# A fused reaction-diffusion and LoRA feed-forward kernel: the first rows of layer 2 by way of DRAM, and two neighbour sums on GpSimd

## The chip, the cores and the metric

The kernel runs on one core of a Trainium2 chip. The metric is the device time of one execution in microseconds (us), as the median of several. TensorE does the matrix products, VectorE and ScalarE the elementwise work, GpSimd some of it and the DMAs that accumulate; SyncE (SP) and ScalarE issue plain DMAs.

## The reference

For each of 8 batches, x is 1024 tokens by 512 features. First a stencil, then a feed-forward layer whose weights have a part that depends on the stencil's own rows 1 to 16, then the residual:

```
y  = zX*(x[t,d-1] - 2x + x[t,d+1]) + zY*(x[t-1,d] - 2x + x[t+1,d]) + zR*x*(1 - x)
even, odd = y[1:17:2], y[2:18:2]             # 8 rows each
m1 = (even[:4] outer odd[:4]) as 2048 x 512  # added to W1
m2 = (even[4:] outer odd[4:]) as 512 x 2048  # added to W2
h  = gelu(y @ (W1 + scale*m1).T + b1)
out = x + h @ (W2 + scale*m2).T + b2
```

(Borders are reflected.) All in float32.

## The kernel before

Products are made from float32 values split into a high and a low part (`yh`/`yl`, `W1h`/`W1l`, `W2h`/`W2l`, `gh`/`gl`), three matmuls of 128x512 for each product, in PSUM. y is computed with features on partitions, in eight tiles a batch: tiles 0 to 3 are the first half of the tokens. The hidden dimension goes in pairs i = 0 to 7 of 128 rows for layer 1 (banks `ph`) and in sixteen tiles n for layer 2 (banks `po`). Batches 1 to 7 repeat one loop; batch 0 has an order of its own, written out by hand for each engine, and the semaphores (`wait_ge`, `then_inc`) tie the engines together. Only the beginning of batch 0 is touched.

The beginning of batch 0 goes so:

- TensorE warms up with 17 matmuls (line 663) and then makes the neighbour sums of y's tile 0 (`raw0`, line 580), `even_row(0)`, the sums of tile 1 (`sums1`), `even_row(1)`, waits for `fold0` and does `pair0(0)`, `even_row(2)`, `pair0(1)`, `pair0(2)` and `pair0(3)` (line 601). `pair0(n)` is the float32 product of W1's first pair of blocks with y's tile n, and waits for that tile (`s_tile`). Then come, at line 630, the six steps of the second pair, which wait for the last part of yh (`s_yht`) and for block 1 of W1h (`s_w1hB`), and at line 694 the first tile of layer 2, which waits for `s_w2h` and, once, for `s_rows2`.
- `even_row(j)` (line 594) spreads a row of four times 128 numbers over all partitions. ScalarE makes diagonal matrices `DE` of the numbers (`diagonals(j)`, line 938), and TensorE multiplies a matrix of ones by them. Row 0 is used for W1's first blocks (`fold0` on VectorE, `outer(0,1)` on ScalarE), row 1 for `outer(0,2)` and `outer(0,3)`, row 2 for W2: ScalarE copies it from PSUM into `EB2` (line 960) and `fold(0, 0)` to `fold(0, 3)` on VectorE (line 1298) add its product with `SC` to the raw W2 tiles.
- The numbers are in `SA`, which VectorE computes in six steps (`scalars0`, the last is `s_sc` 6). Layer 2's later rows come from DRAM: `natural` computes the even rows in another layout, SP stores them to `ep_scratch` and loads them back, broadcast to all partitions (`load_EB2`, into `EB2` or `Ts`).
- A tile n of y needs `scaled(0, n)` on ScalarE (line 787), `mul(0, n)` on VectorE, and the sums of the neighbours in features (`sd`, semaphore `s_md`) and in tokens (`st`, `s_mt`), which `fin` and `tile` on VectorE add. For tile 2 VectorE makes the sums itself (`sums0(2)`, lines 1198 and 1199); for tile 3 GpSimd does (`sums3`, lines 507 and 508), once those of tile 2 are done.
- ScalarE's order: the loads of x tiles 0, 2, 3, 4 (`load_x0`), `scaled` 0 and 1, `diagonals(0)`, `scaled` 2, `diagonals(1)`, `outer(0,1)`, `scaled` 3, `diagonals(2)`, `outer(0,2)`, `outer(0,3)`, the parts yh of tiles 0 and 1 (`part0_h`, line 812), the copy into `EB2`, the parts of tiles 2 and 3, then `w1h_plain(1)` (line 848).
- GpSimd's order: the diagonals of the coefficients, `sums3`, and `add_W1(0, i)`, each a DMA that accumulates the raw W1 blocks onto what `outer(0, i)` has written.
- SP's order: the packed parameters, x tile 1, raw W1 and W2 blocks, `xn`, x tiles 5 to 7, `keep_W1(2)` (which waits for the DMA of `add_W1(0,2)`), two W2 tiles, and so on.

The waits behind `fold` for batch 0 are

```
return ((s_rows2, 1), (d_f1, 16), (d_f2, 16), (d_e2, 16))[j]
```

Of the kernel before, what the change touches and what calls it, by code (L numbers as in the profile page):

```python
# [5 lines left out]
def adaln_ffn_kernel(nc: bass.Bass, xT, xs, x, xn, pk, w1, w2, b2, out):  # L6

    f32 = mybir.dt.float32
    f32r = mybir.dt.float32r
    ALU = mybir.AluOpType  # L10
# [2 lines left out]
    B, S, D = 8, 1024, 512  # L13
    NK, NI = 16, 8
    EP = nc.dram_tensor("ep_scratch", (B * 8, D), f32, kind="Internal").ap()
    UV = nc.dram_tensor("uv_scratch", (NI, 2, 128, 512), f32, kind="Internal").ap()
    TD = nc.dram_tensor("td_scratch", (NI, 128, 512), f32, kind="Internal").ap()

    ctx = ExitStack()
    with ctx:  # L20
# [3 lines left out]
        def sems(names):  # L24
            return [ctx.enter_context(nc.semaphore(n)) for n in names.split()]
# [64 lines left out]
        s_yl = sems(" ".join(f"s_yl{s}" for s in range(7)))  # L90
        d_pk, d_N, d_ep, d_xs = sems("d_pk d_N d_ep d_xs")
        d_keep, d_back = sems("d_keep0 d_keep1"), sems("d_back0 d_back1")
        s_rows2, d_f1, d_f2, d_raw0, d_raw1 = sems("s_rows2 d_f1 d_f2 d_raw0 d_raw1")
        d_e1, d_e2, d_td, d_us, d_vs, d_xr, d_xa = sems("d_e1 d_e2 d_td d_us d_vs d_xr d_xa")
        d_x = sems(" ".join(f"d_x{n}" for n in range(9)))
        d_r, d_q, d_w = sems("d_r0 d_r1"), sems("d_q0 d_q1"), sems("d_w0 d_w1 d_w2 d_w3")
# [78 lines left out]
        def x_at(b, n):  # L175
            x_ = Xs[8 if b else n]
            return [x_[:, r:r + 4, c:c + 128] for r, c in ((1, 1), (0, 1), (2, 1), (1, 0), (1, 2))]

        def sums_at(b, n):
            pair = SS if b else s0[:, n - 1 if n < 4 else n - 3, :, :]  # L180
            return four(pair[:, 0, :]), four(pair[:, 1, :])
# [38 lines left out]
        def rows2_done(b, j):  # L220
            if b:
                return d_e2, 16 * (4 * b + j - 2)
            return ((s_rows2, 1), (d_f1, 16), (d_f2, 16), (d_e2, 16))[j]

        def bank_of(b, h, i, lt):
            if h == 0:
# [7 lines left out]
        def _(e):  # L234
# [7 lines left out]
            def load_x0(n):  # L242
                e.dma_start(Xs[n].rearrange("p r s -> p (r s)"), xT[0, n]).then_inc(d_x[n], 16)
# [59 lines left out]
            def keep_W1(i):  # L303
                e.wait_ge(d_r[i % 2], added(0, i))
                e.dma_start(UV[i].rearrange("h p q -> p h q"),
                            R1[:, i % 2, :, :].rearrange("p (h a) q -> p h (a q)", h=2)).then_inc(d_keep[i % 2], 16)
# [45 lines left out]
            load_W2(0, 0)  # L352
            load_W2(0, 1)
            e.dma_start(xr[:, 0:2, :].rearrange("p a q -> p (a q)"), xn).then_inc(d_N, 16)
            for n in (5, 6, 7):
                load_x0(n)
            keep_W1(2)
            load_W2(0, 2)
            load_W2(0, 3)
# [136 lines left out]
        @block.gpsimd  # L496
        def _(e):
            def diagonal(a, v):
                return e.affine_select(DG[:, a, :], v.broadcast_to([128, 128]), [[-1, 128]],
                                       ALU.is_equal, 0.0, base=0, channel_multiplier=1)  # L500

            def sums3():
                mid, up, down, left, right = x_at(0, 3)
                st, sd = sums_at(0, 3)
                e.wait_ge(d_x[3], 16)
                e.wait_ge(s_mt, 1)
                e.tensor_tensor(sd, up, down, ALU.add).then_inc(s_md, 1)
                e.tensor_tensor(st, left, right, ALU.add).then_inc(s_mt, 1)

            def add_W1(b, i):  # L510
                f = i % 2
                e.wait_ge(s_outer, summed(b, i))
                if (b, i) == (0, 1):
                    e.dma_start(flat(UVs[:, 2:4, :]), w1[1], accum_op=ALU.add).then_inc(d_raw1, 16)
                    return
                e.dma_start(flat(R1[:, f, :, :]), w1[i], accum_op=ALU.add).then_inc(d_r[f], 16)

            def top0(b, i):
                f = i % 2
                if (b, i) > (1, 0):  # L520
                    pb, pi = (b, i - 1) if i else (b - 1, 7)
                    e.wait_ge(d_td, 16 * strassen(pb, pi))
                    e.wait_ge(s_w1lT, strassen(pb, pi))
                e.wait_ge(d_r[f], added(b, i))
                e.tensor_tensor(Ts[:, 0:4:2, :], R1[:, f, 0:1, :].broadcast_to([128, 2, 256]), R1[:, f, 1:3, :],  # L525
                                ALU.subtract).then_inc(s_top0, 1)

            def top1(b, i):
                e.wait_ge(s_top0, strassen(b, i))
                e.tensor_tensor(Ts[:, 1, :], Ts[:, 0, :], R1[:, i % 2, 2, :], ALU.subtract).then_inc(s_top1, 1)  # L530

            def top3(b, i):
                e.wait_ge(s_top1, strassen(b, i))
                e.tensor_tensor(Ts[:, 3, :], Ts[:, 1, :], R1[:, i % 2, 3, :], ALU.add).then_inc(s_top3, 1)

            def add_b2(b, h):
                e.wait_ge(d_xr, 16 * (2 * b + h + 1))
                e.dma_start(xr[:, :, :], bass.AP(b2.tensor, 0, [[0, 128], [0, 4], [1, D]]),
                            accum_op=ALU.add).then_inc(d_xa, 16)

            e.memset(ON[:, :], 1.0).then_inc(s_on, 1)
            e.wait_ge(s_on, 1)
            diagonal(2, ON[:, 0:1]).then_inc(s_sel, 1)
            e.wait_ge(d_pk, 16)
            diagonal(1, zt[:, 0, 1:2]).then_inc(s_dg, 1)
            diagonal(0, zt[:, 0, 0:1]).then_inc(s_dg, 1)
            sums3()
            for i in range(1, NI):
                add_W1(0, i)
            add_b2(0, 0)  # L550
            add_W1(1, 0)
            add_W1(1, 1)
            top0(1, 0)
            top1(1, 0)
            top3(1, 0)
            add_b2(0, 1)
            for b in range(1, B):
                for i in range(7):
                    top0(b, i + 1)
                    top1(b, i + 1)  # L560
                    if i < 6:
                        add_W1(b, i + 2)
                    top3(b, i + 1)
                add_b2(b, 0)
                add_b2(b, 1)
                if b + 1 < B:
                    add_W1(b + 1, 0)
                    top0(b + 1, 0)
                    top1(b + 1, 0)
                    top3(b + 1, 0)  # L570
                    add_W1(b + 1, 1)

        @block.tensor
        def _(e):
# [15 lines left out]
            def even_row(j):  # L590
                for c in range(4):
                    e.wait_ge(s_de, 4 * j + c + 1)
                    bank = (ph[1] if c < 2 else po[2], ph[3], po[3])[j]
                    mm = e.matmul(bank[:, 128 * c:128 * c + 128], ON[:, :], DE[:, j, c, :], start=True, stop=True)  # L594
                mm.then_inc(s_row, 1)

# [70 lines left out]
            even_row(1)  # L667
            e.wait_ge(s_fold1, 1)
            pair0(0)
            even_row(2)  # L670
            for n in range(1, 4):
                pair0(n)

# [14 lines left out]
                mm.then_inc(done, 1)  # L688
            for src, w, ready in ((gh, W2h, s_w2h), (gl, W2h, s_glE), (gh, W2l, s_w2l)):
                e.wait_ge(ready, 1)  # L690
                if ready is s_w2h:
                    e.wait_ge(s_rows2, 1)
                for t in range(4):
                    mm = e.matmul(po[t][:, :], src[:, 0, 128 * t:128 * t + 128], w[:, 1, :], start=w is W2h and src is gh,  # L694
                                  stop=False)
# [80 lines left out]
        def _(e):  # L776
# [152 lines left out]
            def load_x0(n):  # L929
                e.dma_start(Xs[n].rearrange("p r s -> p (r s)"), xT[0, n]).then_inc(d_x[n], 16)  # L930


            def diagonals(j):
                e.wait_ge(s_sel, 1)
                e.wait_ge(s_sc, 6)
                for c in range(4):
                    v = SA[:, c, 2 * j:2 * j + 1] if j < 2 else SA[:, 0, 8 + 2 * c:9 + 2 * c]
                    e.activation(DE[:, j, c, :], DG[:, 2, :], ACT.Copy, scale=v).then_inc(s_de, 1)

            load_x0(0)  # L940
            load_x0(2)
            load_x0(3)
            load_x0(4)
            e.wait_ge(d_pk, 16)
            e.activation(junk[:, :], zt[:, 0, 0:1], ACT.Gelu)
            e.wait_ge(s_zc, 3)
            scaled(0, 0)
            scaled(0, 1)
            diagonals(0)
            scaled(0, 2)  # L950
            diagonals(1)
            outer(0, 1)
            scaled(0, 3)
            diagonals(2)
            outer(0, 2)
            outer(0, 3)
            part0_h(0)
            part0_h(1)
            e.wait_ge(s_row, 3)
            e.activation(EB2[:, :, :].rearrange("p a q -> p (a q)"), po[3][:, :], ACT.Copy).then_inc(s_rows2, 1)  # L960
            part0_h(2)
            part0_h(3)
            w1h_plain(1)
# [185 lines left out]
        def _(e):  # L1149
# [44 lines left out]
            def sums0(n):  # L1194
                mid, up, down, left, right = x_at(0, n)
                st, sd = sums_at(0, n)
                e.wait_ge(d_x[n], 16)
                e.tensor_tensor(sd, up, down, ALU.add).then_inc(s_md, 1)
                e.tensor_tensor(st, left, right, ALU.add).then_inc(s_mt, 1)
# [165 lines left out]
            scalars0()  # L1365
            sums1()
            mul(0, 0)
            sums0(2)
            tile0(0)
            fold0()  # L1370
            mul(0, 1)
# [300 lines left out]
```

## Time and profile before

| | |
|---|---|
| median of 3 runs | 1335.46 us (1335.28 to 1336.07) |
| the profiled execution | 1335.95 us |
| its span, first to last instruction | 1334.7 us |
| granted TensorE clock over the span | 1.000 |
| VectorE, ScalarE, GpSimd busy | 1035.7, 794.3, 256.1 us |
| DMA over the span | 253.52 MB, mean 190 GB/s |

The profile is one execution. The busy times are sums over the instructions; a chain of waits follows the work that ended last back to its start. A matmul's own duration (389 ns for 128x512) contains its pipeline, and the next starts before it ends; in the chain each stands with the time that it adds, 0.23 us. Many instructions of batch 0 overlap by some 0.1 us in the same way.

### The profile page before, as it was taken

The numbers are of one execution on the slowest core, as the hardware profiler recorded it, in microseconds if no ns is written. First come the engines' busy times: TensorE is split into PE (matmuls) and PEld (weight loads), VectorE is DVE, ScalarE is ACT, GpSimd is POOL, SyncE is SP. The second block draws the span as 40 slices with busy tenths as digits, with TensorE's granted clock in tenths as the row PEclk, the third lists the DMA queues.
The fourth block names the chain that finished last, engine by engine and source line by source line (L and its number), as shares of the span: only waits on it lengthen the run. The fifth ranks groups of instructions, "written<-read, shape, count | busy, mean of one in ns | idle before, by whom it ended". The sixth has DMA issues, their size and how long they took to land.

```text
span 1334.7 us, 17125 instructions
## 1 busy us (share of the span) xinstructions
PE 1330.6 (100%) x5901; PEld 1100.4 (82%) x5901; DVE 1035.7 (78%) x1775; ACT 794.3 (60%) x1376; POOL 256.1 (19%) x257
## 2 busy tenths in 40 slices
PE   9999999999999999999999999999999999999999
PEld 7888888888888888888888888888888888888887
DVE  8878799858897688976899768996689967665343
ACT  7654567645775566754577546675467754666432
POOL 1000122301232012320132201331022310232000
PEclk9999999999999999999999999999999999999999
DMA  8765377767778577875868667787767866667661
GB/s 245 195 155 151 81 204 213 203 213 204 180 212 196 189 213 198 203 197 197 208 188 223 183 215 196 193 218 180 224 179 205 214 181 207 161 187 167 176 190 55
DMA packets 140070, 253.52 MB, mean 190 GB/s; under 512 B 13648, under 2 KB 37456, under 8 KB 139984
## 3 DMA queue, kind: packets, MB, share of 16 engines
q1 hardware_dynamic: 121888, 201.03, 47.0%
q0 software_dynamic: 17520, 49.81, 22.5%
q10 hardware_dynamic: 576, 1.60, 0.3%
q8 instruction: 46, 0.75, 0.2%
q14 instruction: 40, 0.33, 0.1%
HBM read 189.34 MB, written 63.05 MB: 189 GB/s over the span
## 4 chain that ended last, share of the span: by engine, by line
PE 100%; DVE 0%; issue 0%; DVEq 0%
PE po L636 17%; PE po L638 17%; PE po L637 17%; PE ph L624 15%; PE ph L620 15%; PE ph L622 15%; PE ph L601 1%; PE ph L630 0%; PE po L580 0%; PE ph L663 0%; PE po L694 0%; DVE xr L1362 0%; PE po L594 0%; PE ph L594 0%; PE po L586 0%; PE po L588 0%
## 5 line engine op out<-in xcount | busy, mean ns | idle before, releaser
L636 PE MATMUL po<-W2h,gh 128*128 128x512 f32 x1020 | 396.8, 389 | 0.0
L637 PE MATMUL po<-W2l,gh 128*128 128x512 f32 x1020 | 396.8, 389 | 0.0
L638 PE MATMUL po<-W2h,gl 128*128 128x512 f32 x1020 | 396.8, 389 | 0.0
L624 PE MATMUL ph<-yh,W1l 128*128 128x512 f32 x896 | 348.6, 389 | 0.0
L622 PE MATMUL ph<-yl,W1h 128*128 128x512 f32 x896 | 348.6, 389 | 0.0
L620 PE MATMUL ph<-yh,W1h 128*128 128x512 f32 x896 | 348.6, 389 | 0.0
L638 PEld LDWEIGHTS po<-W2h,gl 128*128 128x128 f32 x1020 | 191.5, 188 | 39.8
L636 PEld LDWEIGHTS po<-W2h,gh 128*128 128x128 f32 x1020 | 191.5, 188 | 39.7
L637 PEld LDWEIGHTS po<-W2l,gh 128*128 128x128 f32 x1020 | 191.4, 188 | 39.7
L622 PEld LDWEIGHTS ph<-yl,W1h 128*128 128x128 f32 x896 | 168.2, 188 | 35.0
L620 PEld LDWEIGHTS ph<-yh,W1h 128*128 128x128 f32 x896 | 168.2, 188 | 34.9
L624 PEld LDWEIGHTS ph<-yh,W1l 128*128 128x128 f32 x896 | 168.1, 188 | 34.9
L1350 DVE TENSOR_TENSOR gl<-ph,gh 128x512 fp32r<-128x512 f32 x128 | 87.8, 686 | 113.2 <-ACT gh L920 113.1
L525 POOL TENSOR_TENSOR Ts<-R 128x512 f32<-128x512 f32 x56 | 75.5, 1348 | 445.9 <-DVE W1l L1317 380.9
L1355 DVE TENSOR_TENSOR gl<-ph,gh 128x512 fp32r<-128x512 f32 x128 | 87.3, 682 | 79.7 <-ACT gh L927 79.7
L1298 DVE SCALAR_TENSOR_TENSOR W2s<-EB,SC,W2s 128x128 f32<-128x128 f32 x480 | 142.4, 346 | 0.2 <-DMA W2s<-in_w_dram 0.2
L913 ACT ACTIVATE ph<-ph,PK 128x512 f32<-128x512 f32 x128 | 84.1, 657 | 74.4 <-DVE ph L1346 71.9
L1306 DVE TENSOR_TENSOR W2l<-W2s,W2h 128x512 fp32r<-128x512 f32 x124 | 112.2, 905 | 4.2 <-ACT W2h L877 4.1
L920 ACT ACTIVATE gh<-ph 128x512 fp32r<-128x512 f32 x128 | 76.6, 598 | 62.1 <-PE po L638 57.4
L877 ACT ACTIVATE W2h<-W2s 128x512 fp32r<-128x512 f32 x124 | 77.9, 629 | 52.7 <-DVE W2s L1298 52.1
L834 ACT ACTIVATE R<-EB,SC 128x256 f32<-128x256 f32 x240 | 101.8, 496 | 3.1 <-DMA EB<-ep_scratch 3.1
L903 ACT ACTIVATE ph<-ph,PK 128x512 f32<-128x512 f32 x128 | 83.8, 655 | 29.3 <-DVE ph L1340 16.0
(122 smaller groups left out, 1370.2 us busy)
## 6 DMA issues: line engine op xcount, KB each, us to landing
W2s<-in_w_dram SPq DMA_DIRECT2D x124, 256.0 KB, 3.9
R<-in_w_dram POOLq DMA_DIRECT2D x62, 512.0 KB, 7.3
uv_scratch<-UVs SPq DMA_DIRECT2D x112, 256.0 KB, 4.3
UVs<-uv_scratch SPq DMA_DIRECT2D x112, 256.0 KB, 3.9
X<-in_xT_dram SPq DMA_DIRECT2D x56, 390.0 KB, 4.8
xr<-in_x_dram SPq DMA_DIRECT2D x16, 1024.0 KB, 5.5
xr<-in_b_dram POOLq DMA_DIRECT2D x16, 1024.0 KB, 10.6
out_dram<-xr SPq DMA_DIRECT2D x64, 256.0 KB, 2.2
```

Of the source, the lines that this page charges most:

```text
L620: e.matmul(bank[:, :], W1h[:, f, blk, wc], yh[:, q, c, :], start=first and c == 0, stop=False, skip_group_check=not first)
L622: e.matmul(bank[:, :], W1h[:, f, blk, wc], yl[:, q, c, :], start=False, stop=False, skip_group_check=not first)
L624: mm = e.matmul(bank[:, :], W1l[:, f, blk, wc], yh[:, q, c, :], start=False, stop=c == 1, skip_group_check=not first)
L636: e.matmul(po[t][:, :], gh[:, lt, st], W2h[:, k, :], start=i == 0 and lt == 0, stop=False)
L637: e.matmul(po[t][:, :], gh[:, lt, st], W2l[:, k, :], start=False, stop=False)
L638: return e.matmul(po[t][:, :], gl[:, lt, st], W2h[:, k, :], start=False, stop=i == NI - 1 and lt == 1)
L834: m = e.activation(to[:, 2 * h:2 * h + 2, 128 * c:128 * c + 128], row.rearrange("p (a q) -> p a q", a=2), ACT.Copy, scale=SC[:, b % 2, cd, ...
L913: e.activation(bank[:, :], bank[:, :], ACT.Gelu, bias=b1t[:, k:k + 1]).then_inc(s_actL, 1)
L1298: m = e.scalar_tensor_tensor(w, rows2(b, n // 4)[:, a, :], SC[:, b % 2, ck, 4 + a:5 + a], w, ALU.mult, ALU.add)
L1306: e.tensor_tensor(W2l[:, k, :], w2s_at(b, n), W2h[:, k, :].bitcast(f32), ALU.subtract).then_inc(s_w2l, 1)
L1350: e.tensor_tensor(gl[:, 0, :], bank_of(b, h, i, 0)[:, :], gh[:, 0, :].bitcast(f32), ALU.subtract).then_inc(s_glE, 1)
L1355: e.tensor_tensor(gl[:, 1, :], bank_of(b, h, i, 1)[:, :], gh[:, 1, :].bitcast(f32), ALU.subtract).then_inc(s_glL, 1)
```

## The change

Three things are moved in the beginning of batch 0.

1. The row of `even_row(2)`, `diagonals(2)` and the copy from PSUM are gone. ScalarE instead stores the 4 times 128 numbers from `SA` to a new array `row_scratch` in DRAM, right after `scaled(0, 0)`, and SP loads them back, broadcast to all partitions, straight into `EB2`. The first `fold` waits for that load (`d_f0`). TensorE's wait for `s_rows2` goes too.
2. The load of x tile 4 moves from ScalarE's queue to SP's, ahead of tiles 5 to 7.
3. GpSimd makes the neighbour sums of tile 2 too: `side0(2)` (behind `mul(0, 0)`), `token0(2)`, `side0(3)`, `add_W1(0, 1)`, `token0(3)`. VectorE's `sums0(2)` is gone.

```diff
+    R2 = nc.dram_tensor("row_scratch", (4, 128), f32, kind="Internal").ap()
...
-            return ((s_rows2, 1), (d_f1, 16), (d_f2, 16), (d_e2, 16))[j]
+            return ((d_f0, 16), (d_f1, 16), (d_f2, 16), (d_e2, 16))[j]
...
-            for n in (5, 6, 7):
+            for n in (4, 5, 6, 7):
                 load_x0(n)
+            e.wait_ge(d_row2, 16)
+            e.dma_start(EB2[:, :, :], bass.AP(R2.tensor, 0, [[0, 128], [128, 4], [1, 128]])).then_inc(d_f0, 16)
             keep_W1(2)
...
-            def sums3():
-                mid, up, down, left, right = x_at(0, 3)
-                st, sd = sums_at(0, 3)
-                e.wait_ge(d_x[3], 16)
-                e.wait_ge(s_mt, 1)
-                e.tensor_tensor(sd, up, down, ALU.add).then_inc(s_md, 1)
-                e.tensor_tensor(st, left, right, ALU.add).then_inc(s_mt, 1)
+            def side0(n):
+                mid, up, down, left, right = x_at(0, n)
+                e.wait_ge(d_x[n], 16)
+                if n == 2:
+                    e.wait_ge(s_mul, 1)
+                e.tensor_tensor(sums_at(0, n)[1], up, down, ALU.add).then_inc(s_md, 1)
+
+            def token0(n):
+                mid, up, down, left, right = x_at(0, n)
+                e.tensor_tensor(sums_at(0, n)[0], left, right, ALU.add).then_inc(s_mt, 1)
...
-            sums3()
-            for i in range(1, NI):
+            side0(2)
+            token0(2)
+            side0(3)
+            add_W1(0, 1)
+            token0(3)
+            for i in range(2, NI):
                 add_W1(0, i)
...
             pair0(0)
-            even_row(2)
             for n in range(1, 4):
                 pair0(n)
...
                 e.wait_ge(ready, 1)
-                if ready is s_w2h:
-                    e.wait_ge(s_rows2, 1)
...
             load_x0(3)
-            load_x0(4)
...
             scaled(0, 0)
+
+            e.wait_ge(s_sc, 6)
+            e.dma_start(R2.rearrange("c p -> p c"), SA[:, 0, 8:16:2],
+                        allow_slow_non_contiguous=True).then_inc(d_row2, 16)
             scaled(0, 1)
...
             scaled(0, 3)
-            diagonals(2)
             outer(0, 2)
             outer(0, 3)
             part0_h(0)
             part0_h(1)
-            e.wait_ge(s_row, 3)
-            e.activation(EB2[:, :, :].rearrange("p a q -> p (a q)"), po[3][:, :], ACT.Copy).then_inc(s_rows2, 1)
...
             mul(0, 0)
-            sums0(2)
             tile0(0)
```

## Rows read from the trace of the kernel before

**Rows 1.** The page: busy time of TensorE, and the last chain by engine.

```profile
PE 1330.6 (100%) x5901; PEld 1100.4 (82%) x5901; DVE 1035.7 (78%) x1775; ACT 794.3 (60%) x1376; POOL 256.1 (19%) x257
...
PE 100%; DVE 0%; issue 0%; DVEq 0%
```

**Rows 2.** The chain in order of time: start us, us, what.

```profile
9.57 0.45 PE po L594 x4
...
12.63 1.79 PE ph L601 x16
14.42 0.89 PE po L594 x8
15.31 5.36 PE ph L601 x48
20.67 5.49 PE ph L630 x24
...
31.60 0.23 PE ph L620
```

**Rows 3.** Timeline of ScalarE: start us, us, engine, line, what [idle before].

```profile
0.81 1.99 ACTq L930 DMA_DIRECT2D x<-in_xT_dram  x4
...
6.53 0.81 ACT L787 ACTIVATE y<-x,zc 128x512 f32<-128x512 f32 x1 [0.76 <-DMA x<-in_xT_dram]
...
12.41 1.28 ACT L938 ACTIVATE DE<-DG,SA 128x128 f32<-128x128 f32 x4
13.58 2.99 ACT L834 ACTIVATE R<-ph,SC 128x256 f32<-128x256 f32 x8
...
17.47 0.62 ACT L960 ACTIVATE EB<-po 128x512 f32<-128x512 f32 x1
17.95 1.18 ACT L812 ACTIVATE yh<-y 128x512 fp32r<-128x512 f32 x2
18.99 1.09 ACT L848 ACTIVATE W1h<-UVs 128x1024 fp32r<-128x1024 f32 x1
```

**Rows 4.** Timeline of VectorE, the same columns.

```profile
5.90 0.28 DVE L1166 SCALAR_TENSOR_TENSOR SA<-tb,PK,SA 128x64 f32<-128x64 f32 x1
...
8.88 0.69 DVE L1199 TENSOR_TENSOR s<-x 128x512 f32<-128x512 f32 x1
...
10.13 1.66 DVE L1224 SCALAR_TENSOR_TENSOR UVs<-ph,SC,UVs 128x256 f32<-128x256 f32 x4
11.70 0.84 DVE L1253 TENSOR_TENSOR y<-y,x 128x512 f32<-128x512 f32 x1
...
16.94 0.75 DVE L1264 SCALAR_TENSOR_TENSOR y<-s,PK,y 128x512 f32<-128x512 f32 x1
...
23.05 1.13 DVE L1298 SCALAR_TENSOR_TENSOR W2s<-EB,SC,W2s 128x128 f32<-128x128 f32 x4
...
29.38 1.23 DVE L1248 TENSOR_TENSOR W1l<-R,W1h 128x1024 fp32r<-128x1024 f32 x1
...
39.21 1.14 DVE L1298 SCALAR_TENSOR_TENSOR SS<-Ts,SC,SS 128x128 f32<-128x128 f32 x4 [0.84 <-DMA Ts<-ep_scratch]
```

**Rows 5.** Timeline of GpSimd, the same columns.

```profile
9.72 1.28 POOL L507 TENSOR_TENSOR s<-x 128x512 f32<-128x512 f32 x1 [4.83 <-DVE s L1199]
10.96 1.03 POOL L508 TENSOR_TENSOR s<-x 128x512 f32<-128x512 f32 x1
12.13 1.03 POOL L514 DMA_DIRECT2D UVs<-in_w_dram  x1
```

**Rows 6.** DMAs, 0 to 45 us: GB/s in 40 slices; packets, MB, share.

```profile
GB/s 0 40 205 396 401 421 415 403 406 428 397 405 404 209 197 149 153 200 204 222 288 233 15 0 113 229 320 334 66 0 60 202 193 193 350 346 325 284 219 200
...
q10 hardware_dynamic: 576, 1.60, 9.9%
```

**Rows 7.** Line 514, the accumulating DMA of `add_W1(0,1)`: issue to landing.

```profile
DMA to landing us min/median/max: 5.5/5.5/5.5
```

**Rows 8.** Tile EB, 0 to 60 us: its loads from DRAM, issue to landing.

```profile
DMA to landing us min/median/max: 3.1/6.6/9.2
```

More of the change, by code:

```diff
@@ L92, in adaln_ffn_kernel @@
         d_keep, d_back = sems("d_keep0 d_keep1"), sems("d_back0 d_back1")
-        s_rows2, d_f1, d_f2, d_raw0, d_raw1 = sems("s_rows2 d_f1 d_f2 d_raw0 d_raw1")
+        d_row2, d_f0, d_f1, d_f2, d_raw0, d_raw1 = sems("d_row2 d_f0 d_f1 d_f2 d_raw0 d_raw1")
         d_e1, d_e2, d_td, d_us, d_vs, d_xr, d_xa = sems("d_e1 d_e2 d_td d_us d_vs d_xr d_xa")
@@ L592, in even_row @@
                     e.wait_ge(s_de, 4 * j + c + 1)
-                    bank = (ph[1] if c < 2 else po[2], ph[3], po[3])[j]
+                    bank = (ph[1] if c < 2 else po[2], ph[3])[j]
                     mm = e.matmul(bank[:, 128 * c:128 * c + 128], ON[:, :], DE[:, j, c, :], start=True, stop=True)
@@ L936, in diagonals @@
                 for c in range(4):
-                    v = SA[:, c, 2 * j:2 * j + 1] if j < 2 else SA[:, 0, 8 + 2 * c:9 + 2 * c]
+                    v = SA[:, c, 2 * j:2 * j + 1]
                     e.activation(DE[:, j, c, :], DG[:, 2, :], ACT.Copy, scale=v).then_inc(s_de, 1)
```

## Prediction

> **What bounds the kernel now.** I read the page first: TensorE is busy for all but 4 of 1334.7 us, and the chain that ended last is TensorE for 100% of the span [rows 1]. So the only thing that moves the time is TensorE's own work, or a hole in it. Then the chain in order of time [rows 2]: the reader should see that from about 9 us on each piece begins where the one in front of it ends, through the opening (the rows of ones, `pair0`, the block of line 630) into the steady loop. No wait stands between them. The change touches only this opening, so the other views are read for one question: how late may each other engine be before TensorE gets a hole? They are ScalarE's [rows 3], VectorE's [rows 4] and GpSimd's timeline [rows 5], and the DMAs [rows 6 to 8].
>
> **TensorE, removed.** `even_row(2)` is 8 pieces of matmul from 14.42 to 15.31: 0.89 us [rows 2], with `pair0` directly in front and behind. Nothing covers it: it is on the path, and its going is worth at most 0.89 us. TensorE gets nothing new.
>
> **Is TensorE fed 0.89 us earlier?** One fold of `pair0` takes 1.79 us (12.63 to 14.42; the three others 5.36) [rows 2]. Without the row they begin at 12.63, 14.42, 16.21 and 18.00, and line 630 at 19.78 instead of 20.67. What it needs:
> - Tile 3 of y for the last fold. VectorE finishes it at 16.94 + 0.75 = 17.69 [rows 4], needed at 18.00: 0.3 to spare.
> - Block 1 of W1h, from ScalarE, at 19.78; now ready at 18.99 + 1.09 = 20.08 [rows 3]. This one has to move, by 0.3 at least, or the gain is 0.6 instead of 0.89.
>
> **ScalarE, removed and added.** `diagonals(2)`, four copies, 1.28 us (12.41 to 13.69), and the copy of the rows out of PSUM, 0.62 us with 0.48 of it before the next starts (17.47, 17.95) [rows 3]. Added: the issue of the small store, ahead of `scaled(0,1)`. It waits for the last write of SA, 5.90 + 0.28 = 6.18 [rows 4]. ScalarE idles 0.76 us there now, up to 6.53 [rows 3], so the wait is covered. The issue itself: four loads took 1.99 us, 0.50 each [rows 3]; so 6.7 instead of 6.53, 0.15 late. No row shows an issue of single floats. From above I bound it as if each of its 512 floats counted like one of the 144 packets of a load (576 in four [rows 6]): 3.6 times 0.50 = 1.8 us, so up to 1.4 us late; from below by nothing. I take 0.50, since the issues are one instruction each. The load of x tile 4 also leaves this queue, 0.50 less before the table load, which nobody waits for.
> Next, `outer(0,2)` can't simply start 1.28 us earlier: it needs `even_row(1)`, over at 12.63, so it starts at 12.75 instead of 13.58, 0.83 earlier [rows 2, 3]. The eight pieces end at 15.74, the two parts of yh behind them at 16.8, the third at 17.4. The fourth waits for tile 3 (17.69) and takes 0.59 (1.18 for two), to 18.3; W1h follows to about 19.35: 0.7 earlier than now and 0.4 ahead of 19.78. It also needs the accumulating DMA of `add_W1(0,1)`, landed at 12.13 + 5.5 = 17.6 [rows 5, 7].
>
> **VectorE and GpSimd.** VectorE loses `sums0(2)`, two adds of 0.69 in front of 9.5 us [rows 4]. I cost this at nothing: `tile0(0)` behind it needs `raw0`, and `fold0` needs the first row of ones, over at 9.57 + 0.45 = 10.02, and starts at 10.13 already [rows 2, 4]. The freed time becomes idle time ahead of them. GpSimd gets both adds. Its own took 1.28 and 1.03 [rows 5]. It waits for `mul(0,0)`, which stands ahead of the removed adds on VectorE (end near 8.3), so: side 2 from 8.5 to 9.8, token 2 to 10.8, side 3 to 12.1, then `add_W1(0,1)` at 12.1 (it was at 12.13), token 3 from 13.2 to 14.3. `fin(0,2)` and `tile(0,2)` on VectorE come after 13.7, those of tile 3 after 16: more than 1.5 us of cover, and 0 on the path. `token0(3)` is past the DMA issue, so `add_W1(0,1)` isn't behind it, and `add_W1(0,2)` waits for `outer(0,2)` (about 14.2) anyhow.
> What the two engines cost each other: the multiply at 11.70, beside a GpSimd add, took 0.84, 0.15 more than the 0.69 of the plain add [rows 4, 5]. Now about 3.6 us of GpSimd adds lie beside VectorE's work, one of them at a new place (13.2 to 14.3). Two such 0.15 would use up the 0.3 that tile 3 has to spare; four would make a hole of 0.3. Between 0 and 0.3 I take 0.1, since only a part of them comes behind `fold0`.
> The Trainium skill (GPSIMD Engine Reference, Key points) says that GpSimd shares its SBUF interfaces with VectorE and contends with VectorE instructions that have two SBUF inputs. The one multiply fits it. By the rule the three operations of tile 2 beside token 3 stretch as well, 0.45 and with the multiply 0.6: a hole of 0.15 to 0.3 and 1334.8 to 1334.9, where without any contention the sum is 1334.6.
>
> **The DRAM row.** The store issues at about 6.3, into the stretch in which the DMAs run at 390 to 430 GB/s, to about 14.6 us [rows 6]. The ACT queue's packets took 9.9% of 16 engines over 45 us for 576, 0.12 us each; if each float is a packet, with 16 besides as a load has, 528 over 16 engines are 4.1 us. From below, it lands soon after its issue; from above, when that stretch is over. So 8 to 15 us. SP waits for it and then issues the broadcast load, whose like took 3.1 to 9.2 us, median 6.6 [rows 8]: landing between 12 and 24, near 20 if I take the late store and a middling load. VectorE reads the rows in its first `fold`, now at 23.05 [rows 4], then at about 22.3. Behind SP's wait stand `keep_W1(2)` and the loads of W2, which wait for later things still: nothing.
> The Trainium skill (DMA: Bandwidth & Descriptors, Rules for kernel authors) says that a strided last dimension becomes one descriptor for each element. No row here shows such a transfer. By that rule the store is 512 pieces for 2 KB, and lands at the late end of 8 to 15 us rather than at the early one. That speaks against this change, but leaves the sum as it is; only the third rival grows by it.
>
> **Later on.** `w1l_plain(2)` ends at 29.38 + 1.23 = 30.61, and TensorE wants it at 31.4 to 31.6 [rows 2, 4]; even without any shift of VectorE the gain of 0.89 would about hold. `fold(0,4)` at 39.21 waited 0.84 for a DMA [rows 4] which follows `natural` on VectorE, so it shifts along. I see no place that gives the gain back.
>
> **The sum.** Profiled execution 1335.95 (span 1334.7 and 1.25 around it). Less 0.89, plus 0.1 for the later tile 3: 1335.15. The median of the runs, 1335.46, is 0.49 under that execution; on it 0.8 less is 1334.7, and that is the forecast. 0.2% is 2.7 us, about what a measurement can tell from no change here, so even the whole gain is "same".
>
> **The rivals.**
> - ScalarE takes TensorE's place. If the issue of the store takes 1.8 us, `outer(0,1)` and all behind it slip by up to 1.2, W1h comes near 20.1, and 0.3 to 0.6 of the gain are left: 1335.1. For it: 512 single floats; against: four issues of 390 KB each took 0.50, and this is one of 2 KB.
> - The change frees nothing: the time goes into a new wait at tile 3 or at W1h, and TensorE only idles where it worked: 1335.5. Against: two separate covers would have to fail by 0.3 and 0.4.
> - The rows in DRAM come late, the slower side. The place is `fold(0,0)`. It may slip to about 23.0 with what `w1l_plain(2)` has in hand (0.8 from 22.3); each us of landing beyond that is one us of hole in TensorE, whose gain is used up from about 23.8. At the 24.2 of the upper bounds (15 + 9.2) that is +0.4 net, 1335.9; with a store that takes 4 us longer than my upper bound it is 1340. I put the case at 1336.7, a landing near 25.
>
> **How the numbers follow.** Forecast 0.62 (own range 1334.2 to 1335.2), first rival 0.18, second 0.10, third 0.10. The range goes from 1333.8 (full 0.89 and the run to run spread of 1335.28 to 1336.07 on its lower side) to 1336.4, which leaves out most of the third and the edges. Slower by over 2.7 us needs a landing beyond 26.5: 0.03. Faster by over 2.7 us needs three times what is removed: 0.01. Same: 0.96.
>
> **What would show it.** Right: `pair0` as one unbroken 7.15 us and line 630 near 19.8 on the chain; W1h from near 18.3; GpSimd's `add_W1(0,1)` at 12 to 12.4; the broadcast row landed before 22; `fold(0,0)` with no DMA wait. Wrong: an ACT issue over 1 us ahead of `scaled(0,1)`; VectorE or ScalarE waiting for GpSimd's sums at tile 2 or 3; `fold(0,0)` released by the DMA of EB2; a hole in TensorE between 20 and 45 us.

## The result: 8.7 us slower, by a hole in TensorE and a lower clock behind it

| | before | after |
|---|---|---|
| median | 1335.74 us (1335.28 to 1336.36) | 1344.39 us (1343.27 to 1345.21) |
| profiled execution | 1335.95 | 1343.58 |
| its span | 1334.7 | 1342.3 |
| granted TensorE clock | 1.000 | 0.997 |

The ratio of the times is 1.0064 (95% interval 1.0051 to 1.0077), 8.65 us between the medians. The forecast was 1334.7. The page of after shows where to look: TensorE is no longer the whole chain [rows 1], and the first of 40 slices (each digit is a tenth) has lost two tenths of its busy time and a tenth of its clock. Before:

```profile
PE   9999999999999999999999999999999999999999
...
PEclk9999999999999999999999999999999999999999
```

After:

```profile
PE   7999999999999999999999999999999999999999
...
PEclk8999999999999999999999999999999999999999
...
PE 98%; DVE 1%; issue 1%; DVEq 0%
```

The chain of after, in order of time (start, us, what), answers to [rows 2]:

```profile
8.90 0.44 PE ph L604 x4
...
9.89 1.66 DVE UVs L1231 x4
...
13.02 1.54 DVE y L1260
...
18.35 2.05 PE ph L611 x16
20.40 5.86 issue
26.26 7.36 PE ph L640 x24
33.62 2.72 PE po L701 x12
36.34 0.23 PE po L646
```

`pair0` (line 611) ends at 20.40. Before it was 20.67, and the opening began 0.23 later there (line 594 at 9.13 on that chain, 8.90 here), so the removed 0.89 us have left next to nothing: that is one loss. Then TensorE stands for 5.86 us; line 640 (630 before) begins at 26.26, 5.59 later than before. And its 24 matmuls take 7.36 us where they took 5.49, 1.87 more. 5.59 + 1.87 is the 7.46 by which line 646 is late against 636 before (36.34 to 28.88); the spans differ by 7.6. Behind this point next to nothing (0.1 us) is added or given back.

The windows show the clock (columns: window, its length, then busy time and count of TensorE's matmuls and loads, VectorE, ScalarE, GpSimd; granted clock, DMA share, GB/s):

```profile
20.40:26.30 5.90, 0.04 (x2) 0.07 (x1) 0.11 (x1) 1.19 (x2) 0.00 (x0) 0.71 1.07 239
26.30:30.00 3.70, 3.70 (x9) 2.93 (x10) 3.70 (x8) 3.64 (x7) 0.00 (x0) 0.53 1.02 250
...
33.60:36.40 2.80, 2.80 (x14) 2.31 (x13) 2.59 (x6) 0.68 (x2) 0.00 (x0) 1.00 0.81 244
```

While TensorE stood, the clock fell (0.71 in the mean of the hole), and the first 3.7 us of work ran at 0.53, so nearly all at the lower level (1.2 GHz of 2.4): nine matmuls in the time of sixteen.

What TensorE waited for is in ScalarE's timeline and in the DMAs of the first 30 us (GB/s in 40 slices of 0.75 us; issues with their size and time to landing):

```profile
5.74 0.39 ACTq L956 DMA_DIRECT2D row_scratch<-SA  x1
...
6.25 0.81 ACT L794 ACTIVATE y<-x,zc 128x512 f32<-128x512 f32 x1 [0.96 <-DMA x<-in_xT_dram]
...
25.11 1.06 ACT L855 ACTIVATE W1h<-UVs 128x1024 fp32r<-128x1024 f32 x1 [6.15 <-DMA UVs<-in_w_dram]
```

```profile
GB/s 0 0 50 309 329 416 399 406 405 419 388 402 437 389 388 392 250 38 17 33 21 29 33 17 62 108 362 385 210 240 197 219 218 232 238 257 229 235 186 347
...
q10 hardware_dynamic: 960, 1.20, 11.7%
...
x<-in_xT_dram SPq DMA_DIRECT2D x5, 390.0 KB, 15.2
...
UVs<-in_w_dram POOLq DMA_DIRECT2D x1, 512.0 KB, 13.2
EB<-row_scratch SPq DMA_DIRECT2D x1, 256.0 KB, 7.6
row_scratch<-SA ACTq DMA_DIRECT2D x1, 2.0 KB, 15.2
```

Block 1 of W1h (25.11 now, 18.99 in [rows 3]) waited 6.15 us for the accumulating DMA of `add_W1(0,1)`, which landed after 13.2 us instead of 5.5 [rows 7]. It is not alone: from about 12.8 to 18.8 us all DMAs together moved 17 to 62 GB/s, where before they moved some 400 and then 200 [rows 6]. The store of 2 KB took 15.2 us. The loads of x on SP suffered with them: 15.2 us, where they took 9.7 before.

### The profile page after: what moved, and what is told of

The parts are those of the page before. It is cut to its first block, busy times and chain, and to the rows that moved or that the text cites. A ratio compares the mean times of both kernels' runs of the same rounds, so it can differ in the third digit from the quotient of the medians.

```text
span 1342.3 us, 17104 instructions
## 1 busy us (share of the span) xinstructions
PE 1331.9 (99%) x5893; PEld 1101.3 (82%) x5893; DVE 1035.4 (77%) x1773; ACT 794.2 (59%) x1371; POOL 258.7 (19%) x259
## 4 chain that ended last, share of the span: by engine, by line
PE 98%; DVE 1%; issue 1%; DVEq 0%
PE po L646 17%; PE po L648 17%; PE po L647 17%; PE ph L634 15%; PE ph L630 15%; PE ph L632 15%; PE ph L640 1%; PE po L590 0%; PE ph L673 0%; DVE y L1260 0%; PE po L701 0%; DVE xr L1369 0%; PE ph L611 0%; DVE UVs L1231 0%; DVE y L1265 0%
```

## The experiments

Three theories came first. Theory 1: the store of single floats holds up every other DMA, and so W1h. Theory 2: GpSimd's sums make VectorE late, and TensorE loses its clock. Theory 3: the order on SP's queue. Times are medians; the ratio is to the kernel before on the same chip, and where its interval holds 1 the run can't be told from before. The two columns on the right are of the profiled execution: the small store, and the accumulating DMA of `add_W1(0,1)`, which is line 514 before (an edit shifts the line numbers of its run).

| run | median us | ratio, interval | store landed after | line 514's DMA |
|---|---|---|---|---|
| e1, dense store of 512 floats alone | 1344.09 | 1.0064 (1.0049 to 1.0079) | 15.4 | 13.4 |
| e2, 128 pieces of 16 B | 1336.10 | 1.0001 (0.9991 to 1.0010) | 5.9 | 5.7 |
| e3, the change with the old sums | 1344.26 | 1.0064 (1.0049 to 1.0079) | 15.1 | 13.7 |
| e4, GpSimd's sums alone | 1335.90 | 1.0001 (0.9992 to 1.0011) | | 5.7 |
| e5, 512 floats, step 512 B | 1336.08 | 1.0003 (0.9994 to 1.0012) | 8.9 | 5.7 |
| e6, 512 floats into SBUF | 1336.34 | 1.0004 (0.9995 to 1.0013) | 11.1 | 7.2 |
| e7, the row by pieces of 16 B | 1339.25 | 1.0025 (1.0015 to 1.0035) | 6.0 | 7.6 |
| e8, as e1, partition by partition | 1342.21 | 1.0048 (1.0035 to 1.0062) | 13.9 | 10.9 |
| e9, 512 floats, step 64 B | 1335.88 | 1.0000 (0.9991 to 1.0009) | 8.9 | 6.0 |
| e10, 128 floats, dense | 1343.52 | 1.0056 (1.0042 to 1.0069) | 11.8 | 12.0 |
| e11, e2 and the broadcast load | 1336.81 | 1.0009 (1.0000 to 1.0019) | 6.6 | 9.0 |
| e12, the row, loaded later | 1341.03 | 1.0039 (1.0027 to 1.0052) | 6.9 | 5.7 |
| e13, 128 floats, step 16 B | 1336.25 | 1.0002 (0.9992 to 1.0012) | 6.4 | 7.5 |
| e14, 512 floats, step 32 B | 1335.79 | 0.9999 (0.9989 to 1.0009) | 8.8 | 5.8 |
| e15, as e1, at 21.6 us | 1341.31 | 1.0041 (1.0026 to 1.0056) | 10.1 | 5.7 |
| e16, the row left out | 1335.37 | 0.9995 (0.9986 to 1.0004) | | 5.8 |
| e17, e16 with GpSimd's sums | 1335.72 | 1.0000 (0.9991 to 1.0009) | | 6.0 |

### Which part of the change costs

e1 adds only this to the kernel before, and a wait for it far behind:

```diff
...
             scaled(0, 0)
+
+            e.wait_ge(s_sc, 6)
+            e.dma_start(R2.rearrange("c p -> p c"), SA[:, 0, 8:16:2],
+                        allow_slow_non_contiguous=True).then_inc(d_row2, 16)
             scaled(0, 1)
...
             scaled(0, 4)
+            e.wait_ge(d_row2, 16)
             w2h(0, 0)
```

> The kernel before, with nothing but the store of 512 single floats from SA to DRAM added at the place where the change has it; nobody reads what it stores, and ScalarE waits for its landing only ahead of w2h(0,0). Theory 1 (the store holds up every other DMA: in the changed kernel it took 15.2 us and the accumulating DMA of add_W1(0,1) 13.2 instead of 5.5): 7 to 9 us slower, store landed near 21, line 514's DMA at 13 us. Theory 2 (GpSimd's sums make VectorE late and TensorE loses its clock): within 0.5 us of before. Theory 3 (the order on SP's queue, x tile 4 and the broadcast load ahead of the others): within 0.5 us of before.

The DMAs of e1, and its chain:

```profile
UVs<-in_w_dram POOLq DMA_DIRECT2D x1, 512.0 KB, 13.4
row_scratch<-SA ACTq DMA_DIRECT2D x1, 2.0 KB, 15.4
```

```profile
14.82 5.36 PE ph L602 x48
20.18 6.75 issue
26.93 8.12 PE ph L631 x24
```

A store that nobody reads costs 8.4 us, the whole loss, with a like hole (6.75 us) and a like slow block (8.12 us) behind it. e3 takes the change and gives back the sums:

```diff
...
-            side0(2)
-            token0(2)
-            side0(3)
-            add_W1(0, 1)
-            token0(3)
-            for i in range(2, NI):
+            sums3()
+            for i in range(1, NI):
...
             mul(0, 0)
+            sums0(2)
             tile0(0)
```

> The changed kernel with the sums of tile 2 back on VectorE and those of tile 3 after them on GpSimd, as before; the row through DRAM and x tile 4 on SP stay. Theory 1: 7 to 9 us slower than before, the hole in TensorE ahead of line 640 of 5 to 6 us stays. Theory 2: the loss goes, 0.9 us faster than before. Theory 3: as slow as the change.

Nothing is gained back. And e4 is the kernel before with the reverse edit:

> The kernel before with only the sums changed: those of tile 2 on GpSimd too, in the order of the change. Theory 1: 0 to 1 us slower, since a multiply of VectorE beside GpSimd's last add took 1.52 instead of 0.69 in the changed kernel and tile 3 comes later, which now has the 0.9 us of even_row(2) as cover. Theory 2: 7 to 9 us slower.

No measurable difference. Theories 2 and 3 fall as causes of the loss.

### What it is about the store

e2 stores `SA[:, 0, 8:12]`, 128 pieces of 16 B, into `R2` as (128, 4):

> As e1_store_only, but the store is of 128 pieces of 16 B (the same 2 KB, other numbers of SA). Theory 1 with a price for each piece: a quarter of the hold-up of e1_store_only, so about 1.5 us instead of 6, of which block 1 of W1h has 1 us in hand: 0 to 1 us slower. Theory 1 with a price for any small write to DRAM, whatever the number: as slow as e1_store_only. Theories 2 and 3: as before.

```profile
UVs<-in_w_dram POOLq DMA_DIRECT2D x1, 512.0 KB, 5.7
row_scratch<-SA ACTq DMA_DIRECT2D x1, 2.0 KB, 5.9
```

The profiled execution was the fastest of its ten (1335.39). So it isn't any small write. e5 keeps the 512 floats and moves them apart, `R2` as (4, 128, 128) and `R2[:, :, 0]` written; e6 writes them to one partition of `Ts`, not to DRAM:

> As e1_store_only (the kernel before plus 512 stores of one float), but each float goes to a place of its own, 512 B from the next, so that no two pieces meet in the same stretch of DRAM. Theory A (pieces that fall into the same 2 KB of DRAM wait for one another): the hold-up shrinks, store landed by 12, 0 to 2 us slower. Theory B (each piece has its price in the DMA engines, wherever it goes): store at 15 us and 7 to 9 us slower, as e1_store_only.

> As e1_store_only, but the 512 floats go to a row of partition 0 of Ts in SBUF, nothing goes to DRAM. Theory A: as before, within 0.5 us. Theory B: 7 to 9 us slower. A third, C (a piece costs because it is a small write to DRAM, each on its own): as before too, while e5_store_spread stays slow.

Neither can be told from before, though the queue carried the same packets (1104 in e1, e5 and e6: 576 of the loads and 528). Theory B, a price for each piece, falls. e8 writes the dense 2 KB in the order of the partitions:

> As e1_store_only, 512 pieces of one float into 2 KB of DRAM, but in the order in which they are read, so that the four of a partition lie side by side in DRAM and each DMA engine writes its own stretch. Theory A in the form that different engines meet in the same stretch: 0 to 2 us slower. Theory A in any form within an engine, and theory B: as e1_store_only.

It costs 6.5 us instead of 8.4: the order in which the pieces are written matters a little, not much. Then how near is too near? e9 and e14 are e5 with steps of 64 B and 32 B; e10 stores 128 floats densely (`SA[:, 0, 8:9]` into 512 B), and e13 the same floats 16 B apart:

> As e5_store_spread, but each of the 512 floats lies 64 B from the next, all in 32 KB of DRAM. Theory A in the form that pieces disturb one another only within the same 64 B: no cost, as e5_store_spread (within 0.5 us of before, store landed 9 us after its issue). In the form that they disturb one another over hundreds of bytes: 3 to 9 us slower.

> As e1_store_only, but 128 pieces of 4 B side by side in 512 B of DRAM: as many pieces as e2_store_16B, which cost nothing, and as dense as e1_store_only. If density decides, with the price going by the pieces in a stretch: a quarter of the hold-up, 1.5 to 2 us, of which 1 us is covered: 0 to 1.5 us slower, store landed 7 to 9 us after its issue. If only the number of pieces over a threshold counts: as e2_store_16B, 5.9 us and no loss.

> As e9_store_step64 (no cost), but with 32 B between the 512 floats, so two in 64 B. If the price comes from pieces that share 64 B, any number of them: 2 to 8 us slower. If it needs many of them, or a share of the same 32 B: as before.

> As e10_store_128x4B, whose 128 floats lay 4 B apart and cost 7.7 us, but with 16 B from one float to the next, so four pieces in 64 B, as many as e2_store_16B had (which cost nothing with pieces of 16 B). If the number of pieces in the same 64 B decides: as before, within 0.6 us, the DMA of line 514 at 5.5 to 6 us. If it is the size of 4 B together with any neighbour in the 64 B: 4 to 8 us slower.

In the order e10, e14, e13, the DMAs of the first 30 us:

```profile
UVs<-in_w_dram POOLq DMA_DIRECT2D x1, 512.0 KB, 12.0
row_scratch<-SA ACTq DMA_DIRECT2D x1, 0.5 KB, 11.8
```

```profile
UVs<-in_w_dram POOLq DMA_DIRECT2D x1, 512.0 KB, 5.8
row_scratch<-SA ACTq DMA_DIRECT2D x1, 2.0 KB, 8.8
```

```profile
UVs<-in_w_dram POOLq DMA_DIRECT2D x1, 512.0 KB, 7.5
row_scratch<-SA ACTq DMA_DIRECT2D x1, 0.5 KB, 6.4
```

My expectation that a quarter of the dense floats costs a quarter was wrong: 128 of them cost 7.7 us, nearly as much as 512. e13's pieces lie in the same 2 KB as those of e1, and are as many as e10's; what is left is how close they lie. With 16 pieces to each 64 B (e1, e8, e10) the other DMAs are held up; with four (e2, of 16 B each, and e13), two (e14) or one (e9), they aren't, though line 514's DMA took 7.5 us in e13. Between four and sixteen nothing was tried.

e15 issues the store of e1 behind `ghL(0, 0, 0)`, with the wait ahead of `w2h(0, 5)`:

> The dense store of 512 floats of e1_store_only, issued behind ghL(0, 0, 0) at about 22.4 us, when the other DMAs have drained (they move next to nothing from 25 to 27 us in the kernel before); ScalarE waits for it ahead of w2h(0, 5), now at 34 us. If its 15 us are its own and the load of the other queues has no part in them: landed near 37, the W2 loads issued at 26.5 late, TensorE with a hole of several us. If the 15 us come from standing among the 400 GB/s of the opening: landed within 5 us, 0 to 1 us slower than before.

Its DMAs from 15 to 45 us (slices of 0.75 us), and its first late step on VectorE:

```profile
GB/s 197 218 208 98 202 218 191 197 208 213 355 316 20 0 0 0 60 0 85 57 22 49 27 178 407 411 254 45 0 38 52 236 171 221 192 279 367 358 333 331
```

```profile
33.58 1.14 DVE L1303 SCALAR_TENSOR_TENSOR W2s<-EB,SC,W2s 128x128 f32<-128x128 f32 x4 [3.25 <-DMA W2s<-in_w_dram]
```

Landed after 10.1 us, at 31.7, although from 24 us on the other DMAs were all but still. So of e1's 15.4 us at most some 10 are the store's own; the other 5 went with the crowd at the opening. The W2 loads issued at 26.2 moved at 0 to 85 GB/s until it was over. TensorE stood for 2.81 us, and its clock was at the lower level (0.50) for the 5.9 us of work behind that. That the writes into one stretch are done one after the other in the memory, each as a read and a write, would fit, and the Trainium skill (DMA: Bandwidth & Descriptors, Specifications) has read-modify-write for transfers under 512 B; but by that rule alone e2, e9 and e14, whose pieces are as far under 512 B, would be slow too, and no trace here looks inside the memory. This stays open.

### Can the route be saved?

e7 mends the store: ScalarE packs the four columns first, DRAM keeps the order (partition, row), and `fold` reads `EB2` with a step; the sums are the old ones.

```diff
...
+            if (b, j) == (0, 0):
+                return EB2[:, :, :].rearrange("p a q -> p (a q)").rearrange("p (q c) -> p c q", c=4)
...
+            e.activation(SB[:, :], SA[:, 0, 8:16:2], ACT.Copy).then_inc(s_sb, 1)
+            e.wait_ge(s_sb, 1)
+            e.dma_start(R2, SB[:, :]).then_inc(d_row2, 16)
```

> The change's route with a coarser store and the old sums: ScalarE first copies the four columns of SA side by side (128x4), the store is of 128 pieces of 16 B, the row is kept in DRAM in that order, and fold(0, 0) to fold(0, 3) read EB2 with a step of four floats. x tile 4 on SP as in the change. Theory 1 (the pieces of 4 B are the whole loss) and my prediction's sum for TensorE: 0.6 to 0.9 us faster than before, 1334.8 to 1335.1; line 633 of TensorE begins right behind pair0, near 19.8. A rival (the row's wait, or the stepped read of VectorE, eats it): within 0.3 us of before, with a hole in TensorE behind fold.

5 us of the loss are gone, 3.5 are not. Its timeline has two reasons:

```profile
19.93 1.06 ACT L851 ACTIVATE W1h<-UVs 128x1024 fp32r<-128x1024 f32 x1 [1.47 <-DMA UVs<-in_w_dram]
...
23.96 1.50 DVE L1302 SCALAR_TENSOR_TENSOR W2s<-EB,SC,W2s 128x128 f32<-128x128 f32 x4
```

The DMA of `add_W1(0,1)` is still 2 us late, and the stepped read makes four folds 1.50 us instead of 1.13 [rows 4]. The profiled execution was the fastest of the nine, 1337.42; what the others lost on top isn't seen in it. e11 tests the broadcast load by itself, on top of e2, which cost nothing measurable:

```diff
...
+            e.wait_ge(d_row2, 16)
+            e.dma_start(Ts[:, 0:2, :].rearrange("p a q -> p (a q)"), bass.AP(R2.tensor, 0, [[0, 128], [1, 512]])).then_inc(d_f0, 16)
             keep_W1(2)
+            e.wait_ge(d_f0, 16)
...
```

> e2_store_16B, whose store costs nothing, and behind it on SP the load of the 2 KB broadcast to all partitions, into a part of Ts that nobody reads. In e7_row_16B the accumulating DMA of line 514 landed after 7.6 us instead of 5.5, and the DMAs moved only 71 and 85 GB/s for 1.5 us. If the broadcast read does that: line 514's DMA at 7 to 8 us again, W1h ready near 20.9 instead of 20.1, 0 to 0.6 us slower than before. If it was x tile 4 on SP: 5.5 to 6 us, as before.

The median is 1 us above before, and the interval just reaches 1. The profile shows more than that: its execution took 1339.21, one other of the ten 1339.58, and the eight others 1336.5 to 1337.2. In it line 514's DMA took 9.0 us against 5.7 in e2, and its chain reads:

```profile
20.19 1.90 issue
22.09 7.30 PE ph L634 x24
```

The hole is only 1.90 us, and still the clock fell: 0.55 in the mean of the first 3.3 us behind it, and the block took 7.30 us instead of 5.49. Hole and clock come to 3.7 us, of which 0.5 was in hand from an earlier opening (12.15 for the first fold, 12.63 before). The clock over the span agrees: 0.999 in the two longest executions of e11, 1.000 in the eight others. So the load costs some 1 us where the clock holds and over 3 where it falls. In e7 it was 0.999 in three of the nine, 1339.56 to 1340.07; the median, 1339.25, was at 1.000, so the 1.8 us between it and the profiled execution have another cause, which stays open.

e12 lets it wait for that DMA, copies to the right order on ScalarE and puts x tile 4 back:

```diff
...
+            e.wait_ge(d_row2, 16)
+            e.wait_ge(d_raw1, 16)
+            e.dma_start(Ts[:, 0:2, :].rearrange("p a q -> p (a q)"), bass.AP(R2.tensor, 0, [[0, 128], [1, 512]])).then_inc(d_f0, 16)
...
             ghL(0, 0, 0)
+            e.wait_ge(d_f0, 16)
+            e.activation(EB2[:, :, :], Ts[:, 0:2, :].rearrange("p a q -> p (a q)").rearrange("p (q c) -> p c q", c=4),
+                         ACT.Copy).then_inc(s_rows2, 1)
```

> e7_row_16B with its two losses mended: the broadcast load waits for the DMA of add_W1(0,1) and goes to Ts, ScalarE copies it into EB2 in the order that fold reads (0.6 us, behind ghL(0, 0, 0)), and x tile 4 is on ScalarE's queue as before. If the row's DMA traffic and the stepped read are all that e7_row_16B lost: line 514's DMA at 5.5 us, TensorE without a hole up to 30 us and 0.3 to 0.9 us faster than before. If the load, now at 17.7 and some 4 us long, comes too late for fold: a hole in TensorE ahead of layer 2 and 0 to 1 us slower than before.

```profile
25.50 1.11 ACT L973 ACTIVATE EB<-Ts 128x512 f32<-128x512 f32 x1 [3.53 <-DMA Ts<-row_scratch]
...
29.33 1.20 PE L696 MATMUL po<-W2h,gh 128*128 128x512 f32 x4 [3.62 <-ACT W2h L879]
```

```profile
26.00:36.00 10.00, 6.67 (x29) 5.55 (x30) 9.05 (x23) 6.26 (x10) 0.00 (x0) 1.00 0.36 120
```

The second rival of its expectation: issued at 18.27, the load took 7.2 us (I had put 4) and ScalarE, with everything behind it, waited. The window (granted clock 1.00) shows that the clock did not fall in this longer hole. That execution, 1339.76, was the fastest of the five; over the span the clock was 1.000 in it and 0.999 to 0.997 in the four others, 1340.88 to 1342.10. Early the load is in the way of the W1 block, late it is itself too late; a place between the two wasn't tried.

### What the row was worth, and what GpSimd took

e16 leaves the row out altogether (EB2 is set to zero by GpSimd, so the first four W2 tiles lack their added part), and e17 has the change's sums besides.

> The kernel before with layer 2's first rows left out: no even_row(2), no diagonals(2), no copy; GpSimd sets EB2 to zero instead, so the first four W2 tiles lack their added part. No DMA is added. It measures the gain that my prediction counted on, free of the store. The prediction's sum: TensorE's block of line 631 begins 0.89 us earlier, 1335.0. If W1h or tile 3 takes its place: 0.3 to 0.6 us faster only.

> e16_row_left_out with the change's order of sums too (tile 2 on GpSimd). The prediction's sum: 0.1 us slower than e16_row_left_out. By e4_gpsimd_only, where two multiplies of VectorE took 1.59 and 1.53 us beside GpSimd's adds and tile 3 was done near 18.7: the last fold of pair0 waits and most of the 0.89 us goes, 0 to 0.2 us faster than before.

Their chains, e16 first:

```profile
9.44 0.44 PE ph L595 x4
...
12.94 7.15 PE ph L602 x64
20.09 5.49 PE ph L631 x24
```

```profile
9.48 0.44 PE ph L602 x4
...
13.45 1.53 DVE y L1255
...
18.78 2.05 PE ph L609 x16
20.83 5.49 PE ph L638 x24
```

From the first row of ones to the block behind `pair0` it was 20.67 - 9.13 = 11.54 us before; in e16 it is 10.65, in e17 11.35. So the row is worth 0.89 us on the chain, and the sums on GpSimd take 0.70 of it. The medians, 1335.37 and 1335.72 against 1335.96, go the same way, but 0.2% is more than either. The reason is one multiply. GpSimd's last add and VectorE's multiply, in e4:

```profile
12.99 1.36 POOL L511 TENSOR_TENSOR s<-x 128x512 f32<-128x512 f32 x1
```

```profile
13.38 1.53 DVE L1260 TENSOR_TENSOR y<-y,x 128x512 f32<-128x512 f32 x1
```

The multiply of two SBUF tensors lies beside the add for 0.97 us and takes 1.53 instead of 0.69, and tile 3 is 0.7 us later for it. The other multiplies that began beside such an add give the pattern: 0.84 us with 0.29 of overlap [rows 4, 5], 1.59 with 1.05 (e4, 11.08). In all three it is longer by its overlap less 0.14, that is, it ends 0.55 us after the add, whenever it began. The add itself is longer too, 1.36 instead of 1.03.

## Why the prediction was wrong, step by step

- **TensorE, removed.** Right: 0.89 us, and `pair0` as one unbroken 7.15 us in e16, where no store is added.
- **ScalarE.** The issue of the store took 0.39 us against the 0.50 taken, and `scaled(0,1)` still waited for x tile 1; the bound of 1.8 was far off. W1h would have been in time: in e16 it began at 18.41 without waiting for a DMA.
- **"It also needs the accumulating DMA of `add_W1(0,1)`, landed at 12.13 + 5.5 = 17.6."** This is the step that failed. The row of before was carried over as if the added DMAs left it alone. It became 13.2, and that is the hole of 5.86 us. I asked of the store only when it would land, never what it does to those beside it.
- **"if each float is a packet, with 16 besides as a load has, 528 over 16 engines are 4.1 us."** The count was right (960 packets on the queue, 432 of three loads and 528), the price wrong: the pieces of a dense row don't go at the rate of packets of loads. It landed at 20.9 where I had 15 as the latest. The number of packets isn't what decides at all (e9, e14).
- **SP's wait.** The broadcast load was issued at 20.95 and took 7.6 us, landing near 28.5, outside the 12 to 24 given. `fold(0,0)` ran at 29.14, behind a `glE` that was itself late by W1h. The third rival, slower, had the right culprit, and the wrong place: by its rule (a hole from 23.0 on) it would have been 1340.
- **VectorE and GpSimd.** The mechanism was right and its size was not: 0.15 for an overlap, taken from a multiply that had lain beside an add for 0.3 us only; beside one for 1.0 us it is 0.84. With it 0.70 of the 0.89 us go, not 0.1. (The adds were also under-counted: "about 3.6 us" leaves out the last, and the times given come to 4.7. Nothing in the sum rests on it.) The sentences on the Trainium skill (GPSIMD Engine Reference, Key points) made this term a hole of 0.15 to 0.3; even that was short.
- **The clock** stood in no case: 1.87 us of the 7.46. A hole can cost more than its length, and the length alone doesn't tell: it did after 1.90 us in e11's profiled execution, and did not after 3.62 us in e12's.
- **The chances.** 0.96 for "same" came from the thought that the whole edit was worth under 1 us. That bounds the gain, not the loss.

## What to carry to other kernels

A DMA added in a crowded stretch is to be costed by what it does to every transfer beside it, above all to one that the critical engine has little in hand for; the added transfer's own readers may be the smaller matter. Don't gather single floats from many partitions side by side into a row of DRAM; pack them to 16 B first, or set them apart. And take a contention's price from a row with as much overlap as is planned. Scaling 0.15 us for 0.29 of overlap up to 0.97 would have given 0.50, nearer but still short of 0.84; two rows with different overlaps would have shown how it grows.

## What the runs showed of the hardware

- 128 floats written side by side into 512 B of DRAM made the accumulating DMA beside them last 12.0 us instead of 5.5; the same floats 16 B apart 7.5, with no measurable loss in the end, and 512 floats 32 B or 64 B apart 5.8 and 6.0. It held up other queues than its own: the loads of x on SP took 14.5 us instead of 9.7 (e10).
- Where the other DMAs had nearly drained, the dense store of 2 KB still took 10.1 us (e15). Into SBUF it took 11.1 in the crowd of the opening (e6), and all DMAs together kept moving at 300 to 430 GB/s up to 15.7 us.
- Reading one 2 KB row of DRAM into 128 partitions took 4.8 (e11) to 7.8 us (e3), and the accumulating DMA beside it took 9.0 us in e11 against 5.7 in e2, in an execution that took 2.4 us more than the median.
- After 5.86 us without work TensorE's clock was at the lower level for most of the next 3.7 us (0.53 in the mean). In the profiled executions the same followed holes of 1.90 us (e11, 0.55) and 2.81 us (e15, 0.50), but not those of 1.05 us (e7) and 3.62 us (e12), behind which it was 1.00.
- A multiply of two SBUF tensors on VectorE that began beside an add of GpSimd ended 0.55 us after the add, and so took 0.84, 1.53 and 1.59 us instead of 0.69 (before, and twice in e4). An operation of VectorE on 128x512 with one of its inputs in PSUM took 0.69 us wholly beside an add (e17, line 1217, at 9.52), as with none beside it (before, line 1215, at 12.65).
- ScalarE issued a store of 528 packets to DRAM in 0.39 us, and one of 144 in 0.33 (e2); to SBUF the 528 took 0.62 (e6).
